# A graph, attention and expert layer: the order of the setup's loads and norms

## The chip, the cores and the metric

The kernel runs on one core of one Trainium2 chip. The metric is the device time of one execution in microseconds. A time given for a kernel is a median of several runs; durations of single instructions come from one execution under the hardware profiler.

## The reference

The input x has 6250 rows (nodes) of 256 numbers, and there are 200,000 edges, sorted by their destination. The layer normalises x, then adds three things to it.

```python
xn = _layernorm(x, axis=-1)                       # (x - mean) / sqrt(var + 1e-5), without weights
x = x + _L0_gnn_ref(xn, src, dst, edge_type, edge_weight, bases, w_comp) \
      + _L0_mix_ref(xn[None], Wq, Wk, Wv, Wm, W1, W2, g1, b1, g2, b2)[0]
x = x + _L0_ffn_ref(_layernorm(x, axis=-1)[None], Wr, br, W1, b1, ..., Wo, bo)[0]
# gnn: weight[r] = sum_b w_comp[r, b] * bases[b]; out[dst] += (xn[src] @ weight[type]) * edge_weight; relu
# mix: linear attention over the nodes with 8 heads, then a two-layer network, layer norms with g1, b1, g2, b2
# ffn: 8 experts of 256 features; each layer is followed by a batch norm with given statistics
#      (g * (h - m) * rsqrt(v + 1e-3) + b, relu); the experts are weighted by a softmax router
```

## The kernel before, in words

x is cut into 49 tiles of 128 rows. The edges are cut into 1563 chunks of 128; with padding this gives 1968 **steps** in 123 iterations of 16. For each step GpSimd gathers the 128 normed rows that its edges name out of a tensor in the chip's main memory (`normed_nodes`, written `xnD` in the code), TensorE multiplies them by a selection matrix, and VectorE adds the product to a running sum (`pair`, line 1424, two steps at a time). The sums are written out and taken up again by the blocks of expert layers later on.

Every engine runs a list of instructions written out by hand; semaphores (`sem(...)`) hold the lists together. No scheduler moves anything: the order in the source is the order on each engine. ScalarE and SyncE also issue DMAs, each on a queue of its own, and an issue is an instruction in that engine's list: while it waits for room in its queue, nothing behind it starts.

**The setup** is all that comes before the first step:

- SyncE loads `dst` once for a check that the edges really are sorted (`chk_a`, 125 partitions of 1600 numbers and a second small DMA, semaphore `chk_in`), then the first destination of each chunk (`fdst`), then copies the four edge arrays into records in main memory (`rec`, shown as `edge_records`).
- ScalarE issues the loads of x in four groups of 12 tiles (`lnx[0]` to `lnx[3]`, line 815; the last has one tile more, line 818). Group 0 lies in the buffer that the trace calls `mixbuf`, the others in `feed`. Then, before, it issues 28 loads of weights (lines 820 to 838, semaphore `w_in`) and of batch norm vectors (line 840, `bn_in`). After them it norms the groups: for each one a square root over the variances (line 849), a wait for VectorE's scale and shift, 12 or 13 `ACTIVATE`s (line 852) and a store to `normed_nodes` (line 855). After the fourth group it copies the tables of the steps out of PSUM (lines 862 and 863, 16 pairs).
- VectorE checks the order of the edges (lines 1087 and 1134), takes means and variances of group 0 (`ln_stats(0)`, lines 1142 to 1147), counts chunks per tile (up to line 1247), and then does `ln_inverse(0)` (lines 1154 to 1159), which waits for ScalarE's square root. Behind that stands the plan of the steps, up to `cint` (line 1311), for which GpSimd waits before it gathers the edge records (line 783), and `gint`. Then come `ln_stats(1)`, `ln_stats(2)`, `ln_inverse(1)`, `ln_stats(3)`, `ln_inverse(2)`, `ln_inverse(3)` and the split of the gathered records. They are turned on TensorE and copied to the tables by ScalarE.
- The first coefficients (`coefs(0)`), the first selection matrices and, last, `fold_norms()`, which folds the batch norm's statistics into a scale and a shift: 19 VectorE instructions on 16 partitions (lines 1096 to 1105 and the helper's line 1087), with a wait for `bn_in` ahead of them. What it makes is read by TensorE after iteration 16 (`bn_folded`).

**The loop.** Iterations 0 to 16 also run the mix layer's first part, three node tiles in an iteration (`m1_...`); GpSimd spaces its gathers there by a small `memset` every two steps (`calm`), and from iteration 16 to 35 it doesn't. In iteration 16 VectorE also runs `last_steps`, four passes over 2048 numbers and a dozen small instructions. TensorE may run at most a few steps ahead of VectorE's `pair`: a pair of steps waits until all but the last two steps before it have been added (`acc_done`).

Of the kernel before, what the change touches and what calls it, by code (L numbers as in the profile page):

```python
# [9 lines left out]
ACT = mybir.ActivationFunctionType  # L10
# [3 lines left out]
P = 128  # L14
# [84 lines left out]
LG = 4  # L99
# [5 lines left out]
def gps_layer(nc, x, src, dst, etype, eweight, bases, w_comp, Wq, Wk, Wv, Wm, W1, W2, g1, b1, g2, b2,  # L105
              Wr, br, fW1, fb1, fg1, fbe1, fm1, fv1, fW2, fb2, fg2, fbe2, fm2, fv2, Wo, bo, out):
    ctx = ExitStack()
    with ctx:
        sems = {}

        def sem(name):
            if name not in sems:
                sems[name] = ctx.enter_context(nc.semaphore(name))
            return sems[name]
# [199 lines left out]
        def nodes_at(g):  # L314
            return slice(g * LT * P, (g + 1) * LT * P)
# [495 lines left out]
        def _(act):  # L811
            start_ahead(act, "act")

            for g in range(LG):
                act.dma_start(lnx[g][:, 0:LT, :], x[nodes_at(g), :].rearrange("(t p) n -> p t n", p=P)  # L815
                              ).then_inc(sem(f"ln_ld{g}"), 16)
            act.wait_ge(sem("dve_const"), 5)
            act.dma_start(lnx[LG - 1][0:LAST, LT, :], x[(TILES - 1) * P:NODES, :]).then_inc(sem(f"ln_ld{LG - 1}"), 16)
            for q in range(4):
                act.dma_start(wblk[32 * q:32 * q + 32, BASES * q:BASES * (q + 1)], w_comp).then_inc(sem("w_in"), 16)  # L820
            act.dma_start(wq_s, rows(Wq, KH)).then_inc(sem("w_in"), 16)
# [18 lines left out]
                act.dma_start(bnrow[:, n, :], v.rearrange("e (k p) -> (e k) p", p=P)).then_inc(sem("bn_in"), 16)  # L840


            def tiles_of(g):
                return range(g * LT, (g + 1) * LT + g // (LG - 1))

            for g in range(LG):
                act.wait_ge(sem("ln_var"), g + 1)
                ts = tiles_of(g)
                act.activation(lnsq[:, ts[0]:ts[-1] + 1], lnv[:, ts[0]:ts[-1] + 1], ACT.Sqrt).then_inc(sem("ln_root"), 1)
                act.wait_ge(sem("ln_fit"), g + 1)  # L850
                for t in ts:
                    act.activation(lnx[g][:, t - ts[0], :], lnx[g][:, t - ts[0], :], ACT.Identity, bias=lnb[:, t:t + 1],
                                   scale=lnw_[:, t:t + 1]).then_inc(sem("ln_n"), 1)
                act.wait_ge(sem("ln_n"), ts[-1] + 1)
                act.dma_start(xnD[nodes_at(g), :].rearrange("(t p) n -> p t n", p=P), lnx[g][:, 0:LT, :]
                              ).then_inc(sem("ln_st"), 16)
            act.dma_start(xnD[(TILES - 1) * P:TILES * P, :], lnx[LG - 1][:, LT, :]).then_inc(sem("ln_st"), 16)


# [225 lines left out]
        def _(dve):  # L1085
# [252 lines left out]
            def fold_norms():  # L1338
                dve.wait_ge(sem("bn_in"), 160)
                b_, g_, be_, m_, v_ = (bnrow[:, n:n + 6:5, :] for n in range(5))  # L1340
                y = rsqrt(link, v_, BN_EPS, 2 * EXPERTS)
                link(tt(bnt[:, 0:4:2, :], g_, y, ALU.mult))
                link(tt(bnd, b_, m_, ALU.subtract))
                link(tt(bnd, bnd, bnt[:, 0:4:2, :], ALU.mult))
                tt(bnt[:, 1:4:2, :], bnd, be_, ALU.add).then_inc(sem("bn_folded"), 1)
# [63 lines left out]
                dve.wait_ge(sem(f"rels_out{q}"), 16)  # L1409
            link(dve.memset(acc[:, ACCR - 1, :], 0.0))  # L1410
            dve.sem_inc(sem("acc_done"), ALEAD)
            fold_norms()

            def pair(it, p):

# [60 lines left out]
            for it in range(M1_ITS - 1):  # L1476
                for p in range(UN // 2):
                    t = M1_PER * it + M1_AT.index(p) if p in M1_AT else None
                    if t:
                        m1_q(t - 1)  # L1480
                    ahead(it, p, it % SETS)
                    pair(it, p)
                    behind(it, p)
                    if t is not None:
                        m1_plus(t)
                        m1_k(t)
                    if p == 2:
                        split_low(it)


            def last_steps():
# [739 lines left out]
```

## Time and profile before

| | us |
|---|---|
| median of 3 runs | 3489.89 (3484.22 to 3490.11) |
| the profiled execution | 3485.74 |
| its span, first to last instruction | 3484.0 |
| TensorE matmul busy | 2972.8 (85% of the span) |
| VectorE busy | 2232.7 (64%) |
| GpSimd busy | 2069.3 (59%) |
| ScalarE busy | 1000.4 (29%) |

The mean clock granted to TensorE over the span is 0.942 of full speed. The busy shares are means over stages that have different limits: the first steps run on TensorE at 135.83 us, so about 4% of the span is setup, in which TensorE does next to nothing. What ends a wait there has to be read from the timelines of the single engines, in which a bracket at the end of a row gives the idle time before it and who ended it. A row whose engine is written ACTq or SPq is the issue of a DMA, and its length is the time for which the issue held its engine.

### The profile page before, as it was taken

Reading aid. Unit: us, or ns where it says so; the run is one execution under the profiler, and the core shown is the slowest. Engines: PE = TensorE matmul, PEld = TensorE weight load, DVE = VectorE, ACT = ScalarE, POOL = GpSimd, SP = SyncE. Lnnn points to the kernel's source line nnn. Section 1 sums busy time; section 2 is a strip of 40 time slices with the busy share of each in tenths; the row PEclk is TensorE's granted clock in tenths of the full one; section 3 lists DMA queues with packets and bytes.
Section 4 is the critical chain, followed back from the end, with each engine's and each line's share of the span. In section 5 each row is a group of like instructions: output and inputs, shape, how many; then the busy total and the mean of one; then the engine's idle time right before and its main releaser. Section 6 shows DMA issues by size and latency. Waiting matters only on the chain.

```text
span 3484.0 us, 60155 instructions
## 1 busy us (share of the span) xinstructions
PE 2972.8 (85%) x17948; PEld 2623.2 (75%) x17948; DVE 2232.7 (64%) x5862; ACT 1000.4 (29%) x1702; POOL 2069.3 (59%) x2827
## 2 busy tenths in 40 slices
PE   0599996566779999999999999999898999989788
PEld 0477775556668878788888878888787887878677
DVE  4566666555567666767776677667676776766622
ACT  0433331001113323323333323333232332332244
POOL 1466666666566666666666666666666666666500
PEclk9999998677879999999999999999999999999999
DMA  7799997666669888787878888788787888877743
GB/s 178 247 291 303 297 293 231 204 193 208 200 218 284 257 252 257 250 266 254 270 249 258 259 254 271 243 267 254 249 269 243 273 253 252 255 248 252 230 130 130
DMA packets 638070, 852.74 MB, mean 245 GB/s; under 512 B 63579, under 2 KB 515497, under 8 KB 637607
## 3 DMA queue, kind: packets, MB, share of 16 engines
q1 hardware_dynamic: 495087, 536.50, 47.6%
q0 software_dynamic: 95776, 262.27, 25.8%
q10 hardware_dynamic: 46872, 50.02, 4.3%
q8 instruction: 147, 2.41, 0.3%
q14 instruction: 188, 1.54, 0.1%
HBM read 542.52 MB, written 314.58 MB: 246 GB/s over the span
## 4 chain that ended last, share of the span: by engine, by line
PE 56%; issue 15%; DVE 11%; DMA 5%; ACTq 4%; POOL 3%; another core or an unknown queue 3%; ACT 3%; DVEq 0%; POOLq 0%; PEld 0%; PEldq 0%
PE PS L1839 54%; DMA steps<-normed_nodes,steps 5%; DVE steps L1424 4%; POOL steps L798 3%; DVE h_low L1087 1%; DVE steps L1378 1%; DVE feed L1753 1%; PE PS L1909 1%; ACT feed L986 1%; ACT h_high L985 1%; ACTq L815 1%; ACTq L1014 1%; ACTq L1020 1%; DVE feed L1087 1%
## 5 line engine op out<-in xcount | busy, mean ns | idle before, releaser
L798 POOL DMA_INDIRECT steps<-normed_nodes,steps x1968 | 1950.4, 991 | 1112.8 <-issue 545.1
L1424 DVE SCALAR_TENSOR_TENSOR steps<-steps,PS 128x256 f32<-128x256 f32 x1968 | 942.9, 479 | 820.9 <-PE PS L1839 416.2
L1839 PE MATMUL PS<-steps 128*128 128x128 f32 x7872 | 1198.5, 290 | 247.6 <-issue 104.1
L1839 PEld LDWEIGHTS PS<-steps 128*128 128x128 f32 x7872 | 1105.7, 203 | 343.8 <-issue 249.0
L1839 PE MATMUL PS<-bases_s,feed 128*128 128x256 f32 x1568 | 369.8, 380 | 0.5 <-issue 0.5
L986 ACT ACTIVATE feed<-PS,bnc 128x512 f32<-128x512 f32 (+1 forms) x416 | 308.0, 752 | 163.6 <-PE PS L1839 140.5
L1378 DVE TENSOR_TENSOR steps<-steps 128x512 f32<-128x512 f32 x495 | 329.9, 687 | 4.3
L1839 PEld LDWEIGHTS PS<-bases_s,feed 128*128 128x128 f32 x1568 | 287.1, 190 | 35.5 <-issue 1.1
L985 ACT ACTIVATE h_high<-PS,bnc 128x512 fp32r<-128x512 f32 (+1 forms) x208 | 156.7, 753 | 532.6 <-PE PS L1839 315.2
L1839 PE MATMUL PS<-w_one,feed 128*128 128x256 f32 (+1 forms) x980 | 294.3, 433 | 2.2 <-issue 2.2
L1839 PE MATMUL PS<-h_high,split_in 128*128 128x512 f32 (+1 forms) x832 | 249.5, 424 | 9.8 <-ACT feed L986 9.8
L993 ACT COPY feed<-feed 128x1024 f32<-128x1024 f32 x98 | 205.4, 2096 | 162.3 <-DMA feed<-step_sums 155.6
L1839 PE MATMUL PS<-x1t_high,split_in 128*128 128x512 f32 (+1 forms) x832 | 236.8, 406 | 0.0
L1839 PEld LDWEIGHTS PS<-w_one,feed 128*128 128x128 f32 x980 | 174.8, 194 | 42.6 <-issue 29.6
L1839 PE MATMUL PS<-w_zero,feed 128*128 128x256 f32 x784 | 193.4, 381 | 1.4 <-issue 1.4
L1753 DVE SCALAR_TENSOR_TENSOR feed<-PS,rw,feed 128x256 f32<-128x256 f32 x392 | 169.9, 476 | 37.3 <-PE PS L1839 36.8
L943 ACT COPY mixbuf<-PS 128x256 f32<-128x256 f32 x49 | 18.3, 373 | 601.6 <-issue 263.0
L1839 PEld LDWEIGHTS PS<-h_high,split_in 128*128 128x128 f32 x832 | 152.5, 204 | 30.0 <-ACT feed L986 12.0
L1087 DVE TENSOR_TENSOR h_low<-feed,h_high 128x1024 fp32r<-128x1024 f32 (+1 forms) x104 | 120.6, 1160 | 75.2 <-ACT feed L986 75.2
L1839 PEld LDWEIGHTS PS<-feed,w_one 128*128 128x128 f32 x1176 | 148.7, 194 | 26.0 <-issue 26.0
L1839 PE MATMUL PS<-feed,w_one 128*128 128x128 f32 x1176 | 156.3, 276 | 0.0
L1839 PEld LDWEIGHTS PS<-x1t_high,split_in 128*128 128x128 f32 x832 | 144.2, 192 | 15.8
(230 smaller groups left out, 2963.0 us busy)
## 6 DMA issues: line engine op xcount, KB each, us to landing
step_sums<-steps SPq DMA_DIRECT2D x492, 512.0 KB
split_in<-expert_split SPq DMA_DIRECT2D x104, 1024.0 KB
feed<-step_sums SPq DMA_DIRECT2D x392, 128.0 KB
steps<-step_types SPq DMA_DIRECT2D x126, 256.0 KB
steps<-normed_nodes,steps POOLq DMA_INDIRECT x1968
w_zero<-in_L_ffn_Wo_dram SPq DMA_DIRECT2D x52, 256.0 KB
w_one<-in_L_ffn_Wo_dram SPq DMA_DIRECT2D x52, 256.0 KB
mixbuf<-mix_hidden SPq DMA_DIRECT2D x50, 256.0 KB
```

The costliest lines, as they stand in the source:

```text
L798: pool.indirect_dma_start(out=ring[:, k, :], out_offset=None, in_=xnD, in_offset=bass.IndirectOffsetOnAxis(ap=idxc[:, u, k:k + 1], axis=0) ...
L815: act.dma_start(lnx[g][:, 0:LT, :], x[nodes_at(g), :].rearrange("(t p) n -> p t n", p=P)).then_inc(sem(f"ln_ld{g}"), 16)
L985: act.activation(h1_high[:, k, 0:w], bank(b0 + k, 0, w), ACT.Relu, bias=bias, scale=scale)
L986: act.activation(o[:, k, 0:w], bank(b0 + k, 0, w), ACT.Relu, bias=bias, scale=scale).then_inc(sem(f"f_h{s}"), 1)
L993: act.copy(agg[:, h, :, :], at_nodes[:, h, :, :]).then_inc(sem("b_agg"), 1)
L1014: act.load(oregs[0:1], order[0:1, 0, AT[fed] + j:AT[fed] + j + 1])
L1020: act.dma_start(out[bass.ds(full * P, P), :], oacc[:, j, :], cond=(tile < TILES - 1)).then_inc(sem("out_st"), 16)
L1087: return dve.tensor_tensor(o, a, b, op)
L1378: dve.tensor_tensor(selm[:, q, :, :, :], hot[:, s, :].unsqueeze(3).to_broadcast([P, BATCH, GN, BASES]), coef[:, s, :].unsqueeze(2).to_broa ...
L1424: dve.scalar_tensor_tensor(acc[:, k % ACCR, :], acc[:, (k - 1) % ACCR, :], keepc[:, k:k + 1], PS[:, a:a + C], ALU.mult, ALU.add).then_inc( ...
L1753: dve.scalar_tensor_tensor(oacc[:, j, :], o_part(j), rw[:, EXPERTS * j + e:EXPERTS * j + e + 1], oacc[:, j, :], ALU.mult, ALU.add).then_in ...
L1839: return pe.matmul(o, a, b, start=start, stop=stop)
```

## The change

ScalarE's list gets another order. A wait for `chk_in` stands between the load of x group 0 and those of the other groups. The norming of a group is a function, `norm_group(g)`; it is called for group 0 right after the loads of x and ahead of the 28 loads of weights and batch norm vectors, and for groups 1 to 3 after them. On VectorE, `fold_norms()` moves from the end of the setup into iteration 15 of the loop, behind pair 6.

```diff
             for g in range(LG):
+                if g == 1:
+                    act.wait_ge(sem("chk_in"), 32)
                 act.dma_start(lnx[g][:, 0:LT, :], x[nodes_at(g), :]...).then_inc(sem(f"ln_ld{g}"), 16)
             act.wait_ge(sem("dve_const"), 5)
             act.dma_start(lnx[LG - 1][0:LAST, LT, :], x[(TILES - 1) * P:NODES, :]).then_inc(...)
+            def norm_group(g):
+                act.wait_ge(sem("ln_var"), g + 1)
+                ts = tiles_of(g)
+                act.activation(lnsq[...], lnv[...], ACT.Sqrt).then_inc(sem("ln_root"), 1)
+                act.wait_ge(sem("ln_fit"), g + 1)
+                for t in ts:
+                    act.activation(lnx[g][:, t - ts[0], :], ..., ACT.Identity, ...).then_inc(sem("ln_n"), 1)
+                act.wait_ge(sem("ln_n"), ts[-1] + 1)
+                act.dma_start(xnD[nodes_at(g), :]..., lnx[g][:, 0:LT, :]).then_inc(sem("ln_st"), 16)
+
+            norm_group(0)
             for q in range(4):
                 act.dma_start(wblk[...], w_comp).then_inc(sem("w_in"), 16)
...
-            for g in range(LG):
-                (the same body)
+            for g in range(1, LG):
+                norm_group(g)
...
             link(dve.memset(acc[:, ACCR - 1, :], 0.0))
             dve.sem_inc(sem("acc_done"), ALEAD)
-            fold_norms()
...
                     if p == 2:
                         split_low(it)
+                    if p == 6 and it == M1_ITS - 2:
+                        fold_norms()
```

ScalarE's list at its start, before. `mixbuf<-in_x_dram` is the load of group 0, `L849` the square root, `L852` the norms, and `L855` the store.

```order
L815 DMA mixbuf<-in_x_dram 128x12x256
L815 DMA feed<-in_x_dram 128x12x256 x3
L818 DMA feed<-in_x_dram 106x256
L820 DMA feed<-in_L_gnn_w_comp_dram 32x8 x4
L821 DMA w_one<-in_L_mix_Wq_dram 128x2x256
L822 DMA w_one<-in_L_mix_Wk_dram 128x2x256
```

The next 21 loads (`L823` to `L840`) follow, and then the last load and the norms:

```order
L840 DMA feed<-in_L_ffn_v_dram 16x128
L849 ACT_TABLE_LOAD
L849 ACTIVATE steps<-steps 128x12
L852 ACTIVATE mixbuf<-mixbuf,steps 128x256 x12
L855 DMA normed_nodes<-mixbuf 128x12x256
L849 ACTIVATE steps<-steps 128x12
```

The same place in the changed kernel, whose line numbers are higher; `L828` is now the square root, `L831` the norms and `L834` the store:

```order
L817 DMA mixbuf<-in_x_dram 128x12x256
L817 DMA feed<-in_x_dram 128x12x256 x3
L820 DMA feed<-in_x_dram 106x256
L828 ACT_TABLE_LOAD
L828 ACTIVATE steps<-steps 128x12
L831 ACTIVATE mixbuf<-mixbuf,steps 128x256 x12
L834 DMA normed_nodes<-mixbuf 128x12x256
L839 DMA feed<-in_L_gnn_w_comp_dram 32x8 x4
L840 DMA w_one<-in_L_mix_Wq_dram 128x2x256
L841 DMA w_one<-in_L_mix_Wk_dram 128x2x256
```

The table load, the square root, the 12 norms and the store of group 0 now stand ahead of the first weight, and the second group's square root comes behind all 28 small loads.

VectorE's list at the end of the setup, before. The rows on 16 partitions are `fold_norms`, and `L1424` is the first pair of steps:

```order
L1387 TENSOR_TENSOR steps<-steps 128x16
L1410 MEMSET steps 128x256
L1096 TENSOR_SCALAR feed<-feed 16x256
L1097 TENSOR_SCALAR feed<-feed 16x256
L1098 TENSOR_SCALAR feed<-feed 16x256
```

The changed kernel at the same place; `L1430` is the first pair:

```order
L1394 TENSOR_TENSOR steps<-steps 128x16
L1417 MEMSET steps 128x256
L1430 SCALAR_TENSOR_TENSOR steps<-steps,PS 128x256 x2
L1385 TENSOR_TENSOR steps<-steps 128x512
L1094 TENSOR_TENSOR feed<-feed,lnw 128x256
```

The changed kernel's iteration 15, where `L1430` is pair 6 and `L1460` the last instruction of the node tile behind it:

```order
L1430 SCALAR_TENSOR_TENSOR steps<-steps,PS 128x256 x2
L1094 TENSOR_TENSOR feed<-feed,lnw 128x256
L1094 TENSOR_TENSOR feed<-feed 128x256
L1460 SCALAR_TENSOR_TENSOR feed<-feed 128x256
L1103 TENSOR_SCALAR feed<-feed 16x256
L1104 TENSOR_SCALAR feed<-feed 16x256
L1105 TENSOR_SCALAR feed<-feed 16x256
L1094 TENSOR_TENSOR feed<-feed 16x256 x2
L1112 TENSOR_SCALAR feed<-feed 16x256
```

and behind the rest of the folding, where `L1385` is two selection matrices for the next iteration and `L1430` pair 7:

```order
L1094 TENSOR_TENSOR feed<-feed 16x256
L1094 TENSOR_TENSOR feed<-feed 16x2x128
L1094 TENSOR_TENSOR feed<-feed 16x256 x2
L1094 TENSOR_TENSOR feed<-feed 16x2x128
L1385 TENSOR_TENSOR steps<-steps 128x512 x2
L1430 SCALAR_TENSOR_TENSOR steps<-steps,PS 128x256 x2
L1394 TENSOR_TENSOR steps<-steps 128x16
```

The folding stands between pair 6 with its node tile and what leads up to pair 7.

## Rows read from the trace of the kernel before

**Rows 1.** The page's part on the chain that ended last, shares by engine.
```profile
PE 56%; issue 15%; DVE 11%; DMA 5%; ACTq 4%; POOL 3%; another core or an unknown queue 3%; ACT 3%; DVEq 0%; POOLq 0%; PEld 0%; PEldq 0%
```

**Rows 2.** The chain in order of time, start us, us, what; setup.
```profile
3.17 12.19 ACTq L815
15.38 6.88 ACTq L815
22.31 5.59 ACTq L818
27.93 3.39 ACTq L820
```

**Rows 3.** Timeline of ScalarE: start, us, engine, line, op, tiles, count [idle <-releaser].
```profile
1.81 0.44 ACTq L815 DMA_DIRECT2D mixbuf<-in_x_dram  x1
51.53 1.28 ACT L849 ACT_TABLE_LOAD   x1 [51.53 <-issue]
54.36 6.01 ACT L852 ACTIVATE mixbuf<-mixbuf,steps 128x256 f32<-128x256 f32 x12 [1.32 <-DVE steps L1159]
81.56 0.21 ACT L849 ACTIVATE steps<-steps 128x12 f32<-128x12 f32 x1 [21.20 <-DVE steps L1147]
114.84 3.81 ACTq L857 DMA_DIRECT2D normed_nodes<-feed  x1
```

**Rows 4.** Timeline of VectorE in the setup.
```profile
20.54 1.83 DVE L1087 TENSOR_TENSOR steps<-steps 125x1600 f32<-125x1600 int32 x1 [15.86 <-DMA steps<-in_dst_dram]
32.29 0.80 DVE L1247 TENSOR_REDUCE feed<-feed 128x48 f32<-128x624 f32 x1
53.07 0.23 DVE L1154 RECIPROCAL steps<-steps 128x12 f32<-128x12 f32 x1 [19.98 <-ACT steps L849]
86.51 0.22 DVE L1154 RECIPROCAL steps<-steps 128x12 f32<-128x12 f32 x1
```

**Rows 5.** Timeline of SyncE's DMA issues in the setup.
```profile
3.97 14.81 SPq L442 DMA_DIRECT2D fdst<-in_dst_dram  x1
53.98 0.44 SPq L457 DMA_DIRECT2D step_sums<-zrow  x1
```

**Rows 6.** DMA issues of the setup: tile, queue, count, KB each.
```profile
steps<-in_dst_dram SPq DMA_DIRECT2D x1, 781.2 KB
```

**Rows 7.** Stretch: us, busy of five engines (x instructions), PEclk, DMA share, GB/s.
```profile
5.00:10.00 5.00, 0.00 (x0) 0.00 (x0) 0.00 (x0) 0.00 (x0) 0.52 (x2) 1.00 1.09 293
```

**Rows 8.** Timeline of GpSimd, 0 to 160 us.
```profile
75.95 1.02 POOL L783 DMA_INDIRECT steps<-edge_records,cint  x1 [70.30 <-DVE cint L1311]
130.39 0.10 POOL L796 MEMSET hold<- 128x8 f32 x1 [34.64 <-PEq L1891]
```

**Rows 9.** VectorE's groups, 134.6 to 142.4 us: count | busy, mean ns.
```profile
L1087 DVE TENSOR_TENSOR feed<-feed 16x256 f32<-16x256 f32 x13 | 5.4, 416 | 0.4
L1105 DVE TENSOR_SCALAR feed<-feed 16x256 f32<-16x256 f32 x3 | 0.9, 307 | 0.1
```

**Rows 10.** Timeline of TensorE at the loop's start.
```profile
158.16 0.68 PE L1839 MATMUL PS<-steps 128*128 128x128 f32 x4 [3.95 <-DMA steps<-normed_nodes,steps]
```

**Rows 11.** Timeline of VectorE around iteration 15's pairs 6 and 7.
```profile
561.13 0.99 DVE L1424 SCALAR_TENSOR_TENSOR steps<-steps,PS 128x256 f32<-128x256 f32 x2 [13.46 <-remote]
565.61 1.00 DVE L1424 SCALAR_TENSOR_TENSOR steps<-steps,PS 128x256 f32<-128x256 f32 x2 [1.14 <-PE PS L1839]
```

**Rows 12.** Timeline of TensorE, 548 to 600 us.
```profile
570.91 0.61 PE L1839 MATMUL PS<-steps 128*128 128x128 f32 x4
593.45 2.04 PE L1839 MATMUL PS<-steps 128*128 128x128 f32 x8 [12.20 <-DVE steps L1424]
```

**Rows 13.** Stretches of 575 to 592 us, columns as in rows 7.
```profile
575.00:578.00 3.00, 2.27 (x18) 1.95 (x18) 2.90 (x12) 0.00 (x0) 2.09 (x4) 1.00 0.92 251
581.00:592.00 11.00, 0.26 (x3) 0.06 (x1) 10.61 (x16) 0.00 (x0) 4.99 (x6) 0.56 0.74 266
```

**Rows 14.** The chain in order of time, 480 to 760 us.
```profile
739.47 12.89 another core or an unknown queue
```

More of the change, by code:

```diff
@@ L818, in _, with tiles_of @@
             act.dma_start(lnx[LG - 1][0:LAST, LT, :], x[(TILES - 1) * P:NODES, :]).then_inc(sem(f"ln_ld{LG - 1}"), 16)
+            def tiles_of(g):
+                return range(g * LT, (g + 1) * LT + g // (LG - 1))
+            def norm_group(g):
+                act.wait_ge(sem("ln_var"), g + 1)
+                ts = tiles_of(g)
+                act.activation(lnsq[:, ts[0]:ts[-1] + 1], lnv[:, ts[0]:ts[-1] + 1], ACT.Sqrt).then_inc(sem("ln_root"), 1)
+                act.wait_ge(sem("ln_fit"), g + 1)
+                for t in ts:
+                    act.activation(lnx[g][:, t - ts[0], :], lnx[g][:, t - ts[0], :], ACT.Identity, bias=lnb[:, t:t + 1],
+                                   scale=lnw_[:, t:t + 1]).then_inc(sem("ln_n"), 1)
+                act.wait_ge(sem("ln_n"), ts[-1] + 1)
+                act.dma_start(xnD[nodes_at(g), :].rearrange("(t p) n -> p t n", p=P), lnx[g][:, 0:LT, :]
+                              ).then_inc(sem("ln_st"), 16)
+            norm_group(0)
             for q in range(4):
@@ L840, in _ @@
                 act.dma_start(bnrow[:, n, :], v.rearrange("e (k p) -> (e k) p", p=P)).then_inc(sem("bn_in"), 16)
-            def tiles_of(g):
-                return range(g * LT, (g + 1) * LT + g // (LG - 1))
-            for g in range(LG):
[L847 to L856, printed above, removed]
+            for g in range(1, LG):
+                norm_group(g)
             act.dma_start(xnD[(TILES - 1) * P:TILES * P, :], lnx[LG - 1][:, LT, :]).then_inc(sem("ln_st"), 16)
```

## The prediction

> **What bounds the kernel now.** I read the page's chain first, then the chain in order of time over the first 60 us, then the timelines of the five engines in the setup, and last the stretch around 550 us into which a part of VectorE's work moves. The chain as a whole belongs to TensorE [rows 1], but the setup doesn't. There the chain starts on ScalarE's DMA queue: the issues of the x loads hold ScalarE for 12.19, 6.88 and 5.59 us [rows 2], and ScalarE computes nothing until 51.53 us [rows 3]. The reader is to see three numbers together. VectorE has finished all that it can do at 33.09 (32.29 + 0.80), and its next instruction, the reciprocal of group 0, starts at 53.07 after 19.98 us without work, ended by ScalarE's square root [rows 4]. ScalarE gets to that root late for no reason in the data: from 27.93 to 51.53 it issues the 28 loads of weights and batch norm vectors, 23.6 us. Everything behind the reciprocal hangs on VectorE's order: the plan and `cint`, for which GpSimd has waited 70.30 us when it starts at 75.95 [rows 8], the second group's root at 81.56, which ScalarE waited 21.20 us for [rows 3], and then the chain of norms, tables and first coefficients down to the first gather at 130.4 [rows 8]. So microseconds taken out before 53.07 should move the start of the loop one for one, until another list becomes the later one.
>
> **ScalarE's order.** The root of group 0 no longer waits for the 28 loads; it waits until the loads of x are issued. Before, that was at 27.90 (22.31 + 5.59). Now it is later, because groups 1 to 3 wait for the check's data. The price has two parts.
>
> When the check's data lands: before, it was there at 20.54 [rows 4], 17.9 us after its issue at about 2.6, beside three groups of x. Its 781.2 KB [rows 6] came at some 45 GB/s, a small part of the 293 GB/s that all queues moved [rows 7]. Now it has one group beside it, 12 x 128 rows of 1 KB or 1.57 MB. The lower end is both transfers sharing the full rate: 2.37 MB at 293 GB/s is 8.1 us, so 10.7. The upper end is that nothing changes: 20.5. Group 0 alone is through after about 6 us, at 8. If the check moves at 45 GB/s until then (0.24 MB) and the remaining 0.56 MB at 60 to 90 GB/s, it lands between 14.3 and 17.3. I take 16, which is nearer to the one row that shows this transfer.
>
> The Trainium skill speaks against the cheap end. Its page "DMA: Bandwidth & Descriptors", section on why a DMA increments its semaphore by 16, says that a transfer is spread over the largest number of engines up to 16 that divides its outermost dimension; for 125 partitions that is 5 of the 16. The trace agrees so far as 45 GB/s are much less than an equal share of 293. By the rule the other 11 engines stand idle once group 0 is through, and the landing is near 16; without it the landing would be near 10.7 and the sum below 5 us better.
>
> How long the rest of x takes: before, three groups were drained between 1.81 and 27.90, 8.7 us each, when the issue of the last tile was let through. Groups 1 and 2 now stand between the check and that issue: 16 + 2 x 8.7 = 33.4. Ends: at the pace of the two later waits (6.88 and 5.59) 28.5, at that of the first (12.19 each, with the check's data at 20.5) 44.9.
>
> So the table load and root start at 33.4 in place of 51.53: 18.1 us earlier (6.6 to about 24; beyond that VectorE's own work, which ended at 33.09 and gets its data 4.5 us earlier, is the later one). VectorE is free by then, so the reciprocal starts at about 34.9.
>
> **Is ScalarE back in time?** The norms of group 0 ended 8.84 us after the table load's start (54.36 + 6.01 - 51.53) [rows 3]; with 0.4 for the store's issue the loads begin at 42.7. At their full old price of 23.6 us they end at 66.3. Group 1's variances are ready at 81.56 - 18.1 = 63.5, so the root is 2.8 us late, but VectorE asks for it only after the moments of group 2, before at 86.51 [rows 4], now at 68.4. It fits with 2 us to spare. The loads move past a store of 1.57 MB, and an issue behind such a store took 3.81 us [rows 3]; against that, 3.39 us of the 23.6 were one issue of 1 KB held up by x [rows 2]. I count nothing; if both went wrong it costs 2 us. The weights are wanted by VectorE only behind the split of the records, which comes after all four groups' norms are fitted, and are issued by 66 now.
>
> **The other lists.** SyncE's second `fdst` issue was held 14.81 us from 3.97 on, until the check's data was through, and its list of record copies ended near 53.98 [rows 5]. An earlier check moves it forward by about 4 us. GpSimd would want the records at 75.95 - 18.1 = 57.9, when the copies have been issued for 8 us. GpSimd's gathers then have as long as before until VectorE splits them. Nothing here takes the place of the wait. The loop starts 18.1 us earlier.
>
> **The folding.** It is 13 instructions of 0.416 us and 6 of about 0.307 [rows 9], 7.2 us busy and 7.8 with the gaps. At the loop's start it is worth nothing: VectorE was at it while the first gathers, spaced by GpSimd, came in, and TensorE still waited 3.95 us for gathered rows at 158.16, after all of it [rows 10]. In iteration 15 it costs. Pair 6 ran at 561.13 and pair 7 at 565.61 [rows 11]; the 13.46 us without work lie ahead of pair 6, and the folding stands behind it, so they don't cover it. The node tile behind pair 6 ended near 563.3; with 7.8 us of folding and 1.3 for two selection matrices pair 7 starts at 572.4, 6.8 us late. TensorE goes on with two steps and a node tile's products. The third step of iteration 16, which ran at 570.91 [rows 12], needs pair 7 and now waits until 573.4, some 2.5 us. VectorE itself has little air there: it is busy 2.90 of 3 us at 575 and 10.61 of 11 us from 581 to 592, while TensorE waits 12.20 us for it [rows 12, 13]. Of its 6.8 us it makes good the two short waits behind pair 7, so I take 3.2 us. Ends: 0, if it falls into a wait that another engine ends, and 7.8, if nothing covers it.
>
> **The sum**, against the profiled execution's own 3485.74 (span 3484.0): - 18.1 + 0 + 3.2 = - 14.9, so 3470.8. That execution lies 4.15 under the median of 3489.89, so the median of the changed kernel should be 3475.
>
> **Rivals.** *The rest of x comes late.* The check's data gains nothing, and each group needs 12.19 us, since the record copies now run beside all of it: root at 44.9, gain 6.6, folding 3.2, together - 3.4: 3486. For it speaks that idle DMA engines ahead of the check are lost for good; against it that this pace was seen only once and the next two were half of it. 11%.
>
> *The folding costs its full price and ScalarE's list is late by 3.8 us*: - 18.1 + 3.8 + 7.8 = - 6.5: 3483. For it speaks how full VectorE is from 575 to 592. 8%.
>
> *Slower: the folding sets off the long waits.* From iteration 16 on GpSimd's gathers run unspaced, and while they run back to back the other engines have waits of 13 us whose end the trace puts on an unknown queue: 13.46 ahead of pair 6 [rows 11] and 12.89 at 739.47 [rows 14]. Such a wait leaves TensorE at half its clock, and the mean is 0.56 in the stretch from 581 [rows 13]. If VectorE's delay puts the lists out of step so that two more of these fall in, it costs 2 x 13 + 3.2 - 18.1 = + 11: 3501. It decides from the second additional wait. Against it: the spread of three runs is 6 us, so these waits are not thrown by chance from run to run. For it: every time behind the setup moves against the queues. 12%.
>
> *The change does less than it says.* If the records land so late that GpSimd's gathers start no earlier than 75.95, only the 3 us of air behind them are gained: 3489. The 8 us above speak against it. 2%.
>
> **From these the numbers.** My forecast has 65%, between 3464 and 3482. Within 0.2% (7 us, about what a measurement of this kernel can tell from no change) are the first rival, the fourth and, with 2%, a forecast hit by one more long wait, 3475 + 13 = 3488: 15% together. The second rival is just outside, and with the forecast makes faster 73%; slower is the third, 12%. The range goes from 3461, the larger gain of 24 us with a run at the low end of the three, to 3492, which takes in the first two rivals and leaves out the slower one.
>
> **What will show it.** Right: the table load at 33 (28 to 38), the check on VectorE at 16, the reciprocal at 35, GpSimd's first record gather at 58 with VectorE's `cint` ahead of it, first gather of the loop at 112, no folding at the loop's start and TensorE's wait for rows near 140 still there; pair 7 of iteration 15 some 10 us behind pair 6's end, and all times behind iteration 16 earlier by 15. Wrong: a second root that VectorE waits for (then the loads took more than 25 us), a check at 20, or a low clock that lasts longer than before.

## The result

| | us |
|---|---|
| before, median of 20 runs | 3490.00 (3480.59 to 3503.72) |
| changed, median of 20 runs beside them | 3474.70 (3464.74 to 3484.30) |
| ratio | 0.9954, 95% interval 0.9943 to 0.9965 |
| changed, the profiled execution | 3472.93, its span 3471.1 |

The change takes 15.3 us off the median (20 to 12 by the interval); the forecast was 3475. The profiled spans differ by 12.9 us, where the sum said 14.9. The total came out; the terms did so less well: the setup gave 3 us more than forecast, the folding took 1 to 2 us more, and further on the profiled execution lost some 4 us that no term named.

### The profile page after: what moved, and what is told of

The parts are those of the page before. It is cut to its first block, busy times and chain, and to the rows that moved or that the text cites. A ratio compares the mean times of both kernels' runs of the same rounds, so it can differ in the third digit from the quotient of the medians.

```text
span 3471.1 us, 60155 instructions
## 1 busy us (share of the span) xinstructions
PE 2977.1 (86%) x17948; PEld 2628.3 (76%) x17948; DVE 2230.7 (64%) x5862; ACT 999.9 (29%) x1702; POOL 2064.3 (59%) x2827
## 4 chain that ended last, share of the span: by engine, by line
PE 56%; issue 15%; DVE 10%; DMA 6%; POOL 4%; ACTq 3%; ACT 2%; another core or an unknown queue 2%; SPq 1%; DVEq 0%; POOLq 0%; PEld 0%; PEldq 0%
PE PS L1847 55%; DMA steps<-normed_nodes,steps 5%; POOL steps L798 4%; DVE steps L1430 3%; DVE h_low L1094 1%; DVE steps L1385 1%; PE PS L1917 1%; DVE feed L1761 1%; ACT feed L993 1%; DVE feed L1094 1%; ACT h_high L992 1%; ACTq L1027 1%; ACTq L1021 1%; ACTq L1022 0%
## 5 line engine op out<-in xcount | busy, mean ns | idle before, releaser
L1430 DVE SCALAR_TENSOR_TENSOR steps<-steps,PS 128x256 f32<-128x256 f32 x1968 | 942.7, 479 | 827.2 <-PE PS L1847 451.9
L1385 DVE TENSOR_TENSOR steps<-steps 128x512 f32<-128x512 f32 x495 | 329.7, 687 | 4.3
L950 ACT COPY mixbuf<-PS 128x256 f32<-128x256 f32 x49 | 18.2, 372 | 593.1 <-issue 280.2
```

Of the source, the lines that this page charges most:

```text
L1385: dve.tensor_tensor(selm[:, q, :, :, :], hot[:, s, :].unsqueeze(3).to_broadcast([P, BATCH, GN, BASES]), coef[:, s, :].unsqueeze(2).to_broa ...
L1430: dve.scalar_tensor_tensor(acc[:, k % ACCR, :], acc[:, (k - 1) % ACCR, :], keepc[:, k:k + 1], PS[:, a:a + C], ALU.mult, ALU.add).then_inc( ...
```

## The profile of the changed kernel

The chain has the same owners as before [rows 1]; shares by engine:

```profile
PE 56%; issue 15%; DVE 10%; DMA 6%; POOL 4%; ACTq 3%; ACT 2%; another core or an unknown queue 2%; SPq 1%; DVEq 0%; POOLq 0%; PEld 0%; PEldq 0%
```

The chain at its start, in order of time (start us, us, what), answers to [rows 2]:

```profile
3.08 12.81 DMA steps<-in_dst_dram
15.91 0.40 ACTq L817
...
22.20 5.81 ACTq L820
28.04 1.28 ACT L828
```

It starts with the check's data now, and the square root follows the last load of x at once; the 28 loads of weights are gone from it. ScalarE's timeline answers to [rows 3] (`L828` root, `L831` norms, `L839` first weights):

```profile
15.91 6.25 ACTq L817 DMA_DIRECT2D feed<-in_x_dram  x3
28.04 1.28 ACT L828 ACT_TABLE_LOAD   x1 [28.04 <-issue]
30.87 6.01 ACT L831 ACTIVATE mixbuf<-mixbuf,steps 128x256 f32<-128x256 f32 x12 [1.32 <-DVE steps L1166]
37.33 4.84 ACTq L839 DMA_DIRECT2D feed<-in_L_gnn_w_comp_dram  x4
60.04 0.21 ACT L828 ACTIVATE steps<-steps 128x12 f32<-128x12 f32 x1 [23.16 <-issue]
```

The table load moved from 51.53 to 28.04, 23.5 us. The weights' loads and those of the batch norm vectors take 22.7 us (from 37.33 to the next root at 60.04), about the old 23.6, and end before VectorE asks for the second root. VectorE's timeline answers to [rows 4]:

```profile
15.92 1.83 DVE L1094 TENSOR_TENSOR steps<-steps 125x1600 f32<-125x1600 int32 x1 [11.23 <-DMA steps<-in_dst_dram]
27.66 0.80 DVE L1254 TENSOR_REDUCE feed<-feed 128x48 f32<-128x624 f32 x1
29.58 0.23 DVE L1161 RECIPROCAL steps<-steps 128x12 f32<-128x12 f32 x1 [1.12 <-ACT steps L828]
63.02 0.22 DVE L1161 RECIPROCAL steps<-steps 128x12 f32<-128x12 f32 x1
75.44 0.17 DVE L1154 TENSOR_SCALAR steps<-steps 128x13 f32<-128x13 f32 x1 [5.45 <-remote]
100.41 0.25 DVE L1391 CAST steps<-steps 128x16 int32<-128x16 f32 x2 [8.14 <-ACT steps L870]
109.39 0.42 DVE L1373 TENSOR_REDUCE steps<-PS 128x128 f32<-128x256 f32 x1 [8.01 <-PE PS L1847]
120.54 0.99 DVE L1430 SCALAR_TENSOR_TENSOR steps<-steps,PS 128x256 f32<-128x256 f32 x2 [7.56 <-issue]
```

The wait of 19.98 us for the root is now 1.12 us. The reciprocals of groups 0 and 1 come 23.5 us earlier (53.07 to 29.58, 86.51 to 63.02). Then one new wait appears, 5.45 us at 70, and of 23.5 us 21.6 are left at the first reduction of coefficients (130.99 to 109.39). The trace gives it a remote end, and it lies beside GpSimd's record gathers, which run back to back; what ends it isn't shown. Before had six short waits at the same place in the list, 4.9 us together; from group 1's reciprocal to the cast behind the tables it was 35.0 us (86.51 to 121.50) and is 37.4. The last row shows 7.56 us without work ahead of the first pair: the place from which the folding was taken is a wait.

SyncE's and GpSimd's timelines answer to [rows 5] and [rows 8]:

```profile
3.87 11.50 SPq L442 DMA_DIRECT2D fdst<-in_dst_dram  x1
47.53 0.44 SPq L457 DMA_DIRECT2D step_sums<-zrow  x1
```

```profile
55.59 1.03 POOL L783 DMA_INDIRECT steps<-edge_records,cint  x1 [49.94 <-SPq L497]
108.97 0.11 POOL L796 MEMSET hold<- 128x8 f32 x1 [33.58 <-PEq L1899]
```

GpSimd's record gathers begin 20.4 us earlier, ended by SyncE's records and no longer by `cint`, which is ready at 51.6. The last is issued at 74.4, and VectorE splits them only behind the last group's reciprocal at 85.35. The loop starts at 108.97, 21.4 us earlier.

TensorE's wait for gathered rows answers to [rows 10]. It is still there, 21.6 us earlier and as long as before, with no folding ahead of it:

```profile
136.55 1.19 PE L1847 MATMUL PS<-steps 128*128 128x128 f32 x4 [3.84 <-DMA steps<-normed_nodes,steps]
```

How the loads of x went shows in stretches (us, busy of five engines, PEclk, DMA share of 16 engines, GB/s), first of the changed kernel, then of before:

```profile
10.00:15.00 5.00, 0.00 (x0) 0.00 (x0) 0.00 (x0) 0.00 (x0) 0.00 (x0) 1.00 0.32 126
20.00:28.00 8.00, 0.00 (x0) 0.00 (x0) 6.44 (x32) 0.00 (x0) 0.00 (x0) 1.00 1.10 369
```

```profile
10.00:15.00 5.00, 0.00 (x0) 0.00 (x0) 0.00 (x0) 0.00 (x0) 0.00 (x0) 1.00 1.20 222
20.00:28.00 8.00, 0.19 (x2) 0.11 (x2) 7.43 (x14) 0.00 (x0) 0.00 (x0) 1.00 1.04 319
```

With only the check's data under way, a share of 0.32 is busy, 5.1 of 16 engines: the trace agrees with what the Trainium skill says in "DMA: Bandwidth & Descriptors" (section on why a DMA increments its semaphore by 16) of a transfer whose 125 rows split over 5 engines. Behind the check all engines move 369 GB/s. Before, they moved 222 beside the check, and from 20 to 28 us 319, with the engines about as busy. The idle engines of 8 to 16 us did not make the issues later: the last issue of x is through at 28.01, before at 27.90. Not all bytes were made good by then: over the first 28 us the queues moved 221 GB/s on average, before 244, so 0.6 MB less.

In iteration 15 the rows that answer to [rows 11] are pair 6, pair 7 behind the folding, the last pair ahead of iteration 16's reduction of the coefficients, and that reduction:

```profile
535.29 0.99 DVE L1430 SCALAR_TENSOR_TENSOR steps<-steps,PS 128x256 f32<-128x256 f32 x2 [10.87 <-issue]
546.21 0.98 DVE L1430 SCALAR_TENSOR_TENSOR steps<-steps,PS 128x256 f32<-128x256 f32 x2
553.18 1.00 DVE L1430 SCALAR_TENSOR_TENSOR steps<-steps,PS 128x256 f32<-128x256 f32 x2 [1.57 <-PE PS L1847]
554.10 0.42 DVE L1373 TENSOR_REDUCE steps<-PS 128x128 f32<-128x256 f32 x1
```

From pair 6 to the reduction it is 18.81 us, before 14.47 (561.13 to 575.60).

## The experiments

Three sets ran, each on one chip with runs of before beside it; medians of before were 3502.74, 3405.70 and 3394.41 us. So ratios to before are compared across sets, microseconds within one. Two marks serve below: the **first reduction** (the end of the setup) and the **stretch of iteration 15**, from pair 6's start to the next reduction, which stands behind the first three pairs of iteration 16. "Mean difference" is that of the means, with an interval of about 95%.

### First set: the parts apart

**The changed kernel again**, no edit.

> The changed kernel once more, beside the variants. Both theories: ratio to before 0.994 to 0.997; first gather of the loop at 109 us, 21.4 us earlier than before. Theory A (the start of the loop moves one for one, and the stretch of iterations 16 to 40, where GpSimd's gathers run unspaced, scatters by some us from execution to execution): that stretch takes another length than in the first profile of the changed kernel (582.30 to 1010.31 between iteration 17's and iteration 34's reduction of coefficients), by 3 us or more. Theory B (the folding in iteration 15 sets the stretch back each time): the same length within 2 us.

3488.23 us, ratio 0.9957 (0.9943 to 0.9972). First reduction at 109.98, stretch 18.67. The result repeats. Between the reductions of iterations 16 and 33, where the gathers run unspaced, it took 435.9 us, against 429.7 in the first trace of the same kernel: theory A's scatter, though the two traces aren't from one occasion.

**The order of ScalarE without the check's wait and without the folding's move**:

```diff
-                if g == 1:
-                    act.wait_ge(sem("chk_in"), 32)
...
+            fold_norms()                     # at the end of the setup, as before
-                    if p == 6 and it == M1_ITS - 2:
-                        fold_norms()
```

> Group 0 is normed ahead of the weights, but ScalarE does not wait for the check's data and the folding stays at the end of the setup. Theory A: the check's data lands at 20.5 as before, VectorE is free at 33.1 and the reciprocal of group 0 starts there or just behind, 3 to 4 us later than the 29.58 of the changed kernel; GpSimd's record gathers start at 58 to 60 and the loop at 112 to 113. Time about 3 us above the kernel with the wait and the folding at the start: before minus 14. Rival (the wait on the check does nothing): the same start of the loop as with it, 109.

3482.50 us, 0.9947 (0.9928 to 0.9965). ScalarE's and VectorE's timelines:

```profile
3.17 19.38 ACTq L815 DMA_DIRECT2D feed<-in_x_dram  x2
28.26 1.28 ACT L826 ACT_TABLE_LOAD   x1 [28.26 <-issue]
```

```profile
20.88 1.83 DVE L1092 TENSOR_TENSOR steps<-steps 125x1600 f32<-125x1600 int32 x1 [16.20 <-DMA steps<-in_dst_dram]
33.35 0.22 DVE L1159 RECIPROCAL steps<-steps 128x12 f32<-128x12 f32 x1
```

The table load is as early as with the wait (28.26 and 28.04); VectorE is the later one, since its check starts at 20.88, and the reciprocal comes 3.8 us later. The first reduction is at 112.80, 1.9 to 2.8 us later than in the two kernels of this set with the wait. So the order of ScalarE's list makes nearly all of the gain, and the wait 2 to 3 us of it at the first reduction; the medians with and without it, both with the folding at the start, lie 3.7 us apart, within noise.

**The changed kernel with the folding back at the setup's end** (the last three lines of that diff):

> The changed kernel with the folding back at the end of the setup. Theory A: the folding fits into VectorE's wait for the first pair of steps (7.56 us without work ahead of 120.54), so the loop's first pair moves by less than 1 us, and iteration 15 is 2 us shorter; time 2 us under the changed kernel, before minus 17 to 18. Theory B: the folding in iteration 15 also costs 5 us or more in the unspaced stretch behind it; time 6 to 8 us under the changed kernel.

3478.81 us, 0.9934 (0.9919 to 0.9949); mean difference to the changed kernel beside it -7.7 ± 4.1 us. First reduction 110.89, stretch 13.94. The folding stands behind the first reduction, so its price there shows up to the second:

```profile
127.25 0.42 DVE L1373 TENSOR_REDUCE steps<-PS 128x128 f32<-128x256 f32 x1
```

From the first to the second it took 16.36 us, and without the folding 15.72 in the changed kernel beside it and 16.53 in its first trace. At the end the number is theory B's (6 to 8 us under the changed kernel) and not A's (2 us), though the stretch accounts for 4.7 us alone; B's reason is tested by the threefold folding below.

**Before with the folding moved to iteration 15**:

> The kernel before with only the folding moved to iteration 15. Theory A: the loop starts at 130.4 as before, pair 7 of iteration 15 comes 2 to 6 us later, time before plus 2 (ratio 1.0005, within 0.999 to 1.002). Theory B: before plus 6 to 10 (1.002 to 1.003).

3506.76 us, 1.0014 (0.9999 to 1.0028): mean difference to before 3.5 ± 5.2 us. Stretch 18.31. Moving the folding gains nothing by itself, and the interval leaves anything from 2 us of gain to 9 us of loss.

### Second set: the wait alone, the folding's price, the start's worth

**Before, one run**, for a trace of this chip:

> The kernel before once more, for a trace from the same chip as the variants beside it. Theories A (the loop's start moves one for one, the unspaced stretch scatters by itself) and B (the folding in iteration 15 sets later stretches back): first gather at 130.4 and pair 7 of iteration 15 about 4.5 us behind pair 6, as in the first trace. If the length of iterations 17 to 34 (395 us between the reductions in the first trace) differs by more than 5 us, that stretch scatters with no change at all, which theory A needs.

3396.76 us. The first gather was expected at 130.4 and came at 123.3; the first reduction is at 123.86, 7 us earlier than in the first trace of before. Most of the other difference lies in the stretch where the gathers run unspaced. Columns as above, of before in its first trace and in this one:

```profile
600.00:700.00 100.00, 54.97 (x301) 50.14 (x300) 50.01 (x114) 0.00 (x0) 67.83 (x70) 0.69 0.70 198
```

```profile
600.00:700.00 100.00, 67.39 (x400) 61.96 (x400) 66.24 (x161) 2.78 (x7) 76.08 (x79) 0.81 0.79 241
```

In 100 us GpSimd issues 70 gathers on the one and 79 on the other. From iteration 16's to iteration 33's reduction it took 421.5 and 346.1 us; every other stage of the table further down agrees within 12 us. That is a difference between two occasions and doesn't show how far the stretch scatters on one.

**Before with the check's wait alone**:

```diff
+                if g == 1:
+                    act.wait_ge(sem("chk_in"), 32)
                 act.dma_start(lnx[g][:, 0:LT, :], x[nodes_at(g), :]...)
```

> The kernel before with only the wait for the check's data added between the x loads. Both theories: the check's data lands near 16, but VectorE still waits for ScalarE's root, which comes behind the 28 loads: the root at 51.7, the loop's start within 1 us of before, time equal to before within its interval. A rival by which the wait itself costs (DMA engines idle until 16): root and start 3 to 5 us later than before.

3406.27 us, 0.9996 (0.9987 to 1.0005). The check starts at 15.58, and VectorE waits for the root all the longer:

```profile
52.31 0.23 DVE L1156 RECIPROCAL steps<-steps 128x12 f32<-128x12 f32 x1 [24.19 <-ACT steps L851]
```

The first reduction is at 123.49 (before 123.86). The wait is worth something only once the root no longer stands behind the weights.

**The changed kernel with the folding three times in iteration 15**:

```diff
                     if p == 6 and it == M1_ITS - 2:
                         fold_norms()
+                        fold_norms()
+                        fold_norms()
```

> The changed kernel with the folding done three times in a row in iteration 15, 23.4 us of VectorE in place of 7.8. The first times gave the folding there 8 us over the folding at the start. If VectorE's time passes through one for one, this is 15.6 us above the changed kernel: before plus 0 to 1. If each folding upsets the lists behind it (theory B), the unspaced stretch gets longer by more than that, and the time is before plus 5 or more.

3404.80 us, 0.9997 (0.9984 to 1.0010): the whole gain is gone. VectorE:

```profile
521.49 1.00 DVE L1430 SCALAR_TENSOR_TENSOR steps<-steps,PS 128x256 f32<-128x256 f32 x2 [2.31 <-PE PS L1849]
548.10 0.98 DVE L1430 SCALAR_TENSOR_TENSOR steps<-steps,PS 128x256 f32<-128x256 f32 x2
556.09 0.42 DVE L1373 TENSOR_REDUCE steps<-PS 128x128 f32<-128x256 f32 x1
```

The stretch is 34.60 us, 15.9 more than with one folding: the second and third are paid in full, 2 x 7.9. What cover there is, the first one uses up. The unspaced stretch behind it took 343.9 us, against 346.1 in before on this chip, so three foldings didn't set it back: against theory B. At the reduction before this place the kernel was 21.1 us ahead of before, at the one behind it 0.4 behind, and at the end 0.8 ahead (spans).

**The folding at the setup's end, and 23 small memsets on GpSimd ahead of the loop**, meant to take back the earlier start:

```diff
+            pool.wait_ge(sem("mm_done"), 1)
+            for i in range(23):
+                pool.memset(hold[:, :], 0.0).then_inc(sem("spun"), 1)
+                wait_apart(pool, "spun", i + 1)
```

> The changed kernel with the folding back at the end of the setup, and 23 small memsets on GpSimd, one behind the other, ahead of its first gather: about 21 us in which nothing else is moved. Theory A: the loop starts at 130 again and the whole gain of that version (23 us) is given back, time before minus 2 within the interval. A rival (gains in the setup are partly given back in the unspaced stretch anyway, by the moment at which it runs): it costs only 12 to 15 us, time before minus 8 to 11.

3386.09 us, 0.9943 (0.9929 to 0.9956). The memsets came 0.26 us apart, not about 0.9 as expected, so the loop was held for 6.7 us, not 21, and the experiment couldn't cancel the earlier start as it was meant to: neither theory's time (before minus 2, and minus 8 to 11) could be tested. GpSimd:

```profile
100.10 0.10 POOL L804 MEMSET hold<- 128x8 f32 x1 [25.74 <-PEq L1902]
...
106.81 0.10 POOL L796 MEMSET hold<- 128x8 f32 x1 [0.27 <-POOL hold L804]
```

It still tells something. The second reduction was 17.8 us ahead of this chip's before, the reductions of iterations 16 and 119 were 15.5 and 16.6 ahead, the end 13.8 (spans 3395.0 and 3381.2), and the medians lie 19.6 apart. A start so much earlier is kept through the loop, to within the 4 us by which these marks differ.

### Third set: other places for the folding, and one load more moved

**The changed kernel beside them**:

> The changed kernel unedited, beside the three below on one chip. Both theories: 0.4 to 0.5% under before. First theory (the folding costs about what VectorE has no air for in iteration 15): its reductions of the coefficients lose 5 to 8 us between iterations 15 and 17. It is the base that the next three are measured against.

3379.86 us, 0.9958 (0.9945 to 0.9970).

**The folding in iteration 8**:

```diff
-                    if p == 6 and it == M1_ITS - 2:
+                    if p == 6 and it == 8:
```

> The changed kernel with the folding behind pair 6 of iteration 8 instead of 15. First theory (the price is set by how much air VectorE has at the place): in iteration 8 GpSimd still spaces its gathers and sets the pace, so the loss is taken up again within the next two iterations, under 3 us is left at iteration 14, and iteration 15 to 17 show no loss; the kernel is 3 to 6 us under the changed one. Rival (the price is the folding's own 7.8 us wherever the steps run, since every pair waits behind it): the same 5 to 8 us are lost, around iteration 8 instead of 15, and the kernel is the same as the changed one within 2 us.

3376.65 us, 0.9939 (0.9926 to 0.9952). In iteration 15 the stretch is 14.47. In iteration 8 the same stretch is 17.59, and without the folding it is 19.17, 16.62 and 14.71 in the other three kernels of this set. VectorE in iteration 8 with the folding, and then without it, in the kernel told next:

```profile
337.65 1.00 DVE L1430 SCALAR_TENSOR_TENSOR steps<-steps,PS 128x256 f32<-128x256 f32 x2 [2.31 <-PE PS L1847]
350.29 0.99 DVE L1430 SCALAR_TENSOR_TENSOR steps<-steps,PS 128x256 f32<-128x256 f32 x2
355.24 0.42 DVE L1373 TENSOR_REDUCE steps<-PS 128x128 f32<-128x256 f32 x1
```

```profile
340.42 1.00 DVE L1431 SCALAR_TENSOR_TENSOR steps<-steps,PS 128x256 f32<-128x256 f32 x2 [2.31 <-PE PS L1846]
351.66 1.00 DVE L1431 SCALAR_TENSOR_TENSOR steps<-steps,PS 128x256 f32<-128x256 f32 x2 [6.45 <-PE PS L1846]
357.04 0.42 DVE L1373 TENSOR_REDUCE steps<-PS 128x128 f32<-128x256 f32 x1
```

Behind pair 7 VectorE waits 6.45 us for a product of TensorE there, and with the folding not at all: the same instructions fall into that wait, and what they cost is within what the other three kernels differ by. This is the first theory's claim for the place. From iteration 8's reduction to iteration 14's the kernel took 159.6 us and the other three 156.2 to 158.5, so 1 to 3 us may be left. The total doesn't decide: the mean difference to the changed kernel beside it is -1.9 ± 8.7 us.

**The folding in VectorE's wait for the tables**, in the setup:

```diff
+            fold_norms()
             dve.wait_ge(sem("table_cp"), LEAD + 4)
```

> The changed kernel with the folding in VectorE's 8.1 us wait for ScalarE's copies of the tables (92.3 to 100.4 us). First theory: the folding costs nothing there, the loop's first reduction is as early as in the changed kernel (within 0.5 us), nothing is lost between iterations 15 and 17, and the kernel is 5 to 8 us under the changed one, 3464 to 3470 on a chip where the changed one takes 3475. Rival (what is gained ahead of iteration 16 is lost again in the unspaced stretch, and the folding's place is not what decides): the loss of 5 to 8 us is gone at iteration 17 but the end is within 2 us of the changed kernel's.

3379.14 us, 0.9955 (0.9942 to 0.9968). First reduction 102.28 (101.74 in the changed kernel beside it). VectorE in iteration 15 here, and then in the changed kernel beside it:

```profile
524.07 1.00 DVE L1431 SCALAR_TENSOR_TENSOR steps<-steps,PS 128x256 f32<-128x256 f32 x2 [2.20 <-PE PS L1846]
530.70 1.00 DVE L1431 SCALAR_TENSOR_TENSOR steps<-steps,PS 128x256 f32<-128x256 f32 x2 [1.85 <-PE PS L1846]
536.08 0.42 DVE L1373 TENSOR_REDUCE steps<-PS 128x128 f32<-128x256 f32 x1
```

```profile
519.99 1.00 DVE L1430 SCALAR_TENSOR_TENSOR steps<-steps,PS 128x256 f32<-128x256 f32 x2 [2.29 <-PE PS L1847]
538.67 0.42 DVE L1373 TENSOR_REDUCE steps<-PS 128x128 f32<-128x256 f32 x1
```

Stretches of 12.01 and 18.68. At its place the loss is gone, but the time isn't better: the mean difference is +3.7 ± 8.3 us (medians 0.7 apart), where -5 to -8 was expected. That expectation is a miss at the end of the kernel and a hit at the place; at both it is the rival that came out, by which the loss is gone at iteration 17 and the end the same within 2 us. Why the end doesn't follow isn't shown. From iteration 33's reduction to the end, where no edit stands, the four traces of this set took 2481.3 to 2503.2 us, so an effect of 5 us at one place is hard to see there.

**That, and the last tile's load of x behind the norms of group 0**:

```diff
-            act.dma_start(lnx[LG - 1][0:LAST, LT, :], x[(TILES - 1) * P:NODES, :])...   # with its wait, ahead of norm_group(0)
+            act.dma_start(lnx[LG - 1][0:LAST, LT, :], x[(TILES - 1) * P:NODES, :])...   # behind it
```

> As the one before, and the load of x's last tile, whose issue held ScalarE for 5.81 us from 22.20 on, moved behind the norms of group 0. First theory (the root of group 0 waits for ScalarE's issues alone): the table load starts at 22.2 to 24, VectorE's reciprocal not before its own counting is done at 28.5, so 1.1 us earlier than the 29.58 of the changed kernel, the loop's start is 1 us earlier or the same, and the end within 1.5 us of the kernel before it in this list. Rival (the order of the plan on VectorE is not what sets the loop's start any more): no change at all at the loop's start, or a later one by up to 3 us, where the last tile's load comes behind the store of group 0 and holds ScalarE longer.

3376.48 us, 0.9942 (0.9927 to 0.9957). ScalarE, then VectorE:

```profile
22.84 1.28 ACT L826 ACT_TABLE_LOAD   x1 [22.84 <-issue]
25.11 0.21 ACT L826 ACTIVATE steps<-steps 128x12 f32<-128x12 f32 x1 [0.99 <-DVE steps L1154]
```

```profile
28.79 0.22 DVE L1161 RECIPROCAL steps<-steps 128x12 f32<-128x12 f32 x1
```

The table load is 5 us earlier than in the kernel before this one, and the reciprocal 0.6: now VectorE's own counting is the later one, as expected. First reduction 101.72. Nothing more is to be had from ScalarE's order ahead of group 0's root. VectorE's later wait for ScalarE, 7.44 us for the last group's root here and 6.76 in the changed kernel, wasn't tried.

### What the sets say together

| the folding stands in | stretch of iteration 15, us | ratio to before |
|---|---|---|
| iteration 15 (3 kernels) | 18.67 to 18.81 | 0.9954, 0.9957, 0.9958 |
| the setup or iteration 8 (4 kernels, with the new order and the check's wait) | 12.01 to 14.47 | 0.9934, 0.9939, 0.9955, 0.9942 |

All stretches without the folding, before included, lie between 12.0 and 14.5, mostly near 14; with it, in 4 kernels, between 18.3 and 18.8. So its price there is 4 to 5 us (3.8 to 6.8 by the ends). The mean ratios, 0.9956 and 0.9943, differ by 0.0014, 5 us, which agrees in size; but one of the four is no better than the changed kernel, and only within the first set does the interval exclude zero. The best candidate, not a proven one, is the changed kernel with the folding left where it was.

## Why the prediction was right, and where not

- *The root of group 0 is free once the x loads are issued, and VectorE stands waiting for it.* Right, and it is nearly the whole gain. Shown by the order alone (0.9947) and by the wait alone (0.9996).
- *The check's data at 16.* Right: 15.92, and with it 5 of 16 engines busy. The two paces behind the number were wrong in opposite ways, which is luck: alone, the check's data moved at 126 GB/s, not 60 to 90. In the first 10 us all queues together moved 1.75 MB, of which group 0 is 1.57, so the check had got at most 0.2 MB by then, where the forecast's paces give 0.4.
- *Two more groups of x need 2 x 8.7 us, so the root comes at 33.4.* Wrong by 5.3 us: from the check to the end of the last issue it took 12.1 us, not 17.4, so the table load came at 28.04, 23.5 us earlier, not 18.1. It lay within the bounds named (28.5 was the early end, missed by 0.5). The pace of 8.7 us was an average that contained the first issue of 12.19 us; before's two later ones together took 12.5 (6.88 and 5.59), the pace that came. Without the wait the table load came at 28.26, so the root was not made later by it, as the forecast had it.
- *VectorE is free by then.* Right, with 1.12 us to spare.
- *ScalarE is back in time.* Right: weights issued at 59.99, root 60.04, VectorE's next reciprocal without a wait.
- *GpSimd's record gathers at 58 with `cint` ahead of it.* The time nearly right (55.59), the order wrong: the records were the later, by 4 us. It cost nothing at the split, for which VectorE is ready only at 86.5.
- *The loop starts earlier one for one.* Nearly: 23.5 became 21.4. The 2.1 us went into VectorE's wait of 5.45 us, which wasn't in the sum; the same kernel had 4.60 us there in the first set and none in the third, and the kernels of the second set had none either.
- *At the loop's start the folding is worth 0.* Nearly: about 1 us. From the first to the second reduction it took 16.4 to 17.5 us with the folding and 15.7 to 16.5 without it in the six traces of the slower occasions, and on the second set's chip 18.2 and 18.0 with it against 17.0 without. With it put back, the kernel was faster.
- *In iteration 15 it costs 3.2.* Mis-sized: 4 to 5 us. It was priced as 7.8, less 1.1 ahead of pair 7, less two waits of 3.06 and 0.50 behind it. Pair 7 came 10.92 us behind pair 6, before 4.48: late by 6.4, as forecast (6.8). But only about 2 of the 3.6 us were made good, because TensorE, itself held up by VectorE's pairs, is late with the last product (the 1.57 us wait at 553). Its row there:

```profile
551.76 1.13 PE L1847 MATMUL PS<-steps 128*128 128x128 f32 x8 [0.61 <-DVE steps L1430]
```
- *The sum.* Two errors of 3 and 1 us had opposite signs, and with them alone the sum would be about - 17. That it came within 1 us of the median is in part luck. What else moved is in this table of stages, in us of the profiled executions (iterations by their reductions):

| stage | before | changed | difference | the changed kernel again |
|---|---|---|---|---|
| start to the first reduction | 131.0 | 109.4 | -21.6 | 110.0 |
| to iteration 14 | 380.7 | 381.6 | +0.9 | 380.3 |
| to iteration 16, with the folding | 63.9 | 63.1 | -0.8 | 71.0 |
| to iteration 33, unspaced | 421.5 | 429.7 | +8.2 | 435.9 |
| to the end | 2486.9 | 2487.3 | +0.4 | 2486.9 |

The 4.3 us that the folding costs are in the third row, where shorter waits with a remote or unnamed end (10.87 for 13.46, and others) take them back, and 8.2 us are lost in the fourth, where no edit stands. In six traces on the two slower occasions the fourth stage took 421.5 and 425.6 us with ScalarE's old order (before, and before with the folding moved) and 426.3, 429.7, 432.9 and 435.9 with the new one. So on these occasions the earlier start may give some of itself back there. On the two faster occasions there is no such order: 346.1 and 349.4 with the old one, 343.9 to 349.4 with the new one. The same program differed by 6.2 us from one slower occasion to the other. Scatter of the unspaced gathers and a loss that comes with the earlier start both stay open.

The rivals: the rest of x wasn't late (root at 28.04, not 44.9), ScalarE's list wasn't either, and the record gathers began at 55.59, not 75.95 (that rival's own sum, - 3 + 3.2, gives 3490, not 3489). The slower rival, long waits set off by the folding, didn't occur: one wait of 10.87 us stands ahead of pair 6, where before had 13.46, and between the reductions of iterations 16 and 33 VectorE has four waits of over 5 us, 23 us together, where before had six of 40 us, none of them over 9.

## What to carry to other kernels

Look for an engine that waits long for one small instruction, and see what stands ahead of it in the other engine's list: issues of loads that nobody wants yet cost as much as computing. Work that is moved off an idle place is no gain; put it where its engine waits longer than it lasts, and count of the waits behind it only those that don't depend on it. A wait that holds back a queue can be free: here the loads behind it were all issued by 28 us, with it and without it.

## What was not expected of the hardware

- Loads behind a lone transfer run faster than the same loads beside it: 369 GB/s from 20 to 28 us against 222 from 10 to 15 us, beside the check's data, with a DMA share of 1.10 and 1.20. Before, too, the rate rose once the check was through, to 379 GB/s from 26 to 28 us. Which of the transfers lowers the rate per engine wasn't tried.
- Before took 3490, 3503, 3406 and 3394 us on the four occasions. Of the 89 us between the trace of the first occasion and that of the second set (spans) 75 lie where gathers run unspaced (421.5 against 346.1 us), and on the faster ones VectorE's long waits of iteration 15 (10.87 to 17.13 us in five of the six slower traces) are missing. What makes the two differ stays open.
- The issue of a single tile of x, 106 KB, held ScalarE for 5.81 us behind three loads of 1536 KB, and for 2.49 us where it stood behind the norms of group 0.
- On GpSimd a memset of 8 numbers a partition behind another, with a wait between them, starts 0.26 us after it.
